# A four-layer state-space image block on one Trainium2 core: z computed beside the layer norm's statistics, the scan's first block made a stage earlier, and y's columns gathered by ScalarE

## The chip, the cores and the metric

The kernel runs on one core of one Trainium2 chip. The metric is the device time of one execution, in microseconds. The kernel before takes 28529.37 us (median of 3 runs, 28515.41 to 28530.03). The times of the profile come from one more, profiled execution of 28593.1 us, whose profiled span is 28591.4 us.

## The reference

Four images of 64 x 64 pixels and 192 channels pass through four layers one after the other. Layers 0 to 2 are selective-scan blocks; layer 3 is a block in which the four directions fall together, so that it needs no scan. For each layer and image, cut to what matters:

```
x  = group_norm(x_in)                        # 32 groups, over the whole image
xi, z = split(x @ in_proj.T)                 # 384 + 384 channels; z = silu(z)
xi = silu(depthwise_conv3x3(xi) + bias)      # layers 1, 2 and 3 alone
# four directions k: rows, columns, rows backwards, columns backwards
dts, B, C = split(x_proj[k] @ xs[k])         # rank + 16 + 16 rows
dt = softplus(dt_proj[k] @ dts + dt_bias[k])
h  = exp(dt * A[k]) * h + (dt * xs[k]) * B   # over 4096 positions, 16 states
y[k] = sum_n h[n] * C[n] + D[k] * xs[k]
y  = y[0] + columns_to_rows(y[1]) + flip(y[2]) + columns_to_rows(flip(y[3]))
y  = layer_norm(y) * w + b                   # over the 384 channels
x_out = x_in + (y * z) @ out_proj.T
```

Everything is float32.

## The kernel before

Channels lie on the partitions, positions along the free axis in 8 chunks of T = 512. The 384 inner channels are three blocks `d` of 128. A loop on the device runs over the 4 images; in it, layer by layer, stand three stages, each ended by a barrier of all engines: `norm_conv`, then `scan`, then `out_gated` (layer 3 has no scan and ends with `out_proj`). So one execution has 16 `norm_conv`, 12 `scan`, 12 `out_gated` and 4 `out_proj`. Each engine's instructions stand in an order written out by hand, and engines wait for each other by counting semaphores; nothing is planned at run time.

`norm_conv` (from L240) takes the group norm's statistics, projects xi (`project_in`, L535), convolves it where there is a convolution (taps on TensorE and VectorE) into `u`, and projects dts, B and C (`project_x`, L558), which ScalarE copies out of PSUM (`keep_x`, L468). SyncE stores them to DRAM: directions 0 and 2 chunk by chunk (`store_even`), directions 1 and 3, transposed, in one go at the end (`store_odd`, L323). SyncE then waits for all of the even stores and for the first chunk's dts, B (`diag`) and C (`c_all`), which it has loaded in the meantime (L359 to L364).

`scan` (from L605) works through 4 directions of 8 chunks of 3 blocks d: 96 units. A unit has 8 steps `g` of 2 states each. In each step TensorE multiplies dt*u with B (`inputs`, L717, into PSUM), ScalarE makes exp(dt*A) (`make_decays`, L842), VectorE runs two scans (`scans`, L918), ScalarE keeps the last column (`keep_last`, L835), GpSimd multiplies with C (`weigh`, L965, waits for `keep_last`), and TensorE sums the product by transposing matmuls (`sums`, L735) three steps later (`PE_LAG`). The next unit's dt is made in between: TensorE's `project_dt` (L697) at g = 1 behind `sums`, ScalarE's `softplus_in` and `softplus_log` at g = 2 and 3, VectorE's `make_dt` after the scans of g = 3, GpSimd's `make_dtu` at g = 3, TensorE's `turn_dtu` (L708) at g = 6, ScalarE's `keep_turned` (L818) at g = 7. The unit before is finished at the same time: `keep_yT` at g = 3, TensorE's `start_y` (L750) at g = 4, `turn_y` at g = 5, ScalarE's `keep_y` (L860) at g = 6. `start_y` adds what y holds so far (an identity matmul over `y_acc`, or in direction 0 the D weights `skip_w` over `u`); in directions 1 and 3 its moving operand is read by columns, 256 bytes from one element to the next. At g = 4 of each chunk's first unit ScalarE issues the two DMAs of `spread` (L826), which bring the next chunk's B into place. Ahead of the first unit stand, in a row: a table load, the three `skip_w` weights (L870), `project_dt`, the softplus, `make_dt`, `make_dtu`, `turn_dtu` and `keep_turned` of unit 0.

`out_gated` (from L986) loads x (two halves), the input weights and the output weights. It first runs the statistics over y's channels: VectorE's `sum_y` and `centre`, TensorE's `mean` (L1011) and `variance` (L1018) by a matmul with a constant matrix, ScalarE's `squares` and `deviation`, GpSimd's sum of squares. z is projected by `project_z` (L1025) on x normalised by ScalarE (`normalise`, L1080); two of the eight chunks lie within the statistics, the other six between the output projections (`project_out`, L1038). ScalarE's `silu` goes from PSUM into `u`, and VectorE's `scale`, `gate` and `add_x` make the result. All `project_out` share one pair of PSUM banks.

## Time and profile before

| what | us |
|---|---|
| median of 3 runs | 28529.37 |
| profiled execution | 28593.1 |
| its profiled span | 28591.4 |
| TensorE matmul busy | 27059.4 (95%) |
| VectorE busy | 25875.7 (91%) |
| GpSimd busy | 23415.0 (82%) |
| ScalarE busy | 18929.7 (66%) |
| one scan of twelve (image 0, layer 0, first to last scan instruction) | 1963.8 |

PE is TensorE's matmul side, PEld its weight load, DVE VectorE, ACT ScalarE, POOL GpSimd, SP SyncE (SPq are the DMAs that it issues). The busy shares are means over stages with different limits, so each stage is to be read by itself. A row of the windows view has the stretch and its length, then the busy time (and instructions) of PE, PEld, DVE, ACT and POOL, the granted TensorE clock, the DMA engines' share and GB/s. A row of the timeline has start, length, engine, line, operation, what it writes and reads, how many in a run, and in brackets how long its engine stood idle and what ended that.

### The profile page before, as it was taken

To read this page: it belongs to the slowest core of one execution; us is meant where nothing else is said; L and a number is where in the kernel's file an instruction comes from. 1 tells how busy PE (TensorE), PEld (TensorE's weight loads), DVE (VectorE), ACT (ScalarE), POOL (GpSimd) and SP (SyncE) were. 2 spreads that over 40 slices of the span, in tenths; PEclk is the share of its full clock that TensorE was granted. 3 is DMA by queue.
4 is the path that set the end of the run, shared out by engine and by line. 5 is a ranking of instruction groups with operands and counts; after the bars stand their busy time and mean duration, and the time that the engine had idled before them with its cause. 6 is when DMAs were issued, how large, how long until landed. Compare 5 with 4: busy or idle time off the path is not lost. (4 is left out here: it accounts for less than half of the span.)

```text
span 28591.4 us, 600844 instructions
## 1 busy us (share of the span) xinstructions
PE 27059.4 (95%) x242880; PEld 20043.6 (70%) x242880; DVE 25875.7 (91%) x24430; ACT 18929.7 (66%) x37728; POOL 23415.0 (82%) x10688
## 2 busy tenths in 40 slices
PE   8999998998999999899899999989989999998998
PEld 6776775774677677577467767757746776775774
DVE  8998997997899899899789989979978998997997
ACT  6775775774677577577467757757746775775774
POOL 7996995994799699599479969959947996995994
PEclk9999999999999999999999999999999999999999
DMA  3332332331333233233133323323313332332331
GB/s 106 102 101 80 105 105 80 106 110 44 101 104 100 82 103 105 80 109 108 45 100 105 99 82 102 105 80 108 108 45 100 105 99 82 102 105 80 108 108 45
DMA packets 3552030, 2679.50 MB, mean 94 GB/s; under 512 B 3255348, under 2 KB 3258636, under 8 KB 3294584
## 3 DMA queue, kind: packets, MB, share of 16 engines
q1 hardware_dynamic: 489912, 2628.56, 25.9%
q10 hardware_dynamic: 3059328, 12.24, 6.2%
q8 instruction: 1934, 31.69, 0.5%
q14 instruction: 856, 7.01, 0.1%
HBM read 2541.99 MB, written 111.15 MB: 93 GB/s over the span
## 5 line engine op out<-in xcount | busy, mean ns | idle before, releaser
L971 POOL TENSOR_TENSOR regB<-regB,regA 128x1024 f32<-128x1024 f32 x9216 | 21517.9, 2376 | 618.8 <-ACT carry L838 607.4
L932 DVE TENSOR_TENSOR_SCAN regB<-regB,carry,ps 128x512 f32<-128x512 f32 x16128 | 19137.1, 1257 | 243.6 <-PE ps L730 215.8
L849 ACT ACTIVATE regB<-regB,a_neg 128x512 f32<-128x512 f32 x18432 | 12184.1, 710 | 0.6 <-issue 0.2
L730 PEld LDWEIGHTS ps<-regA,regB 64*128 64x128 f32 x147456 | 8999.2, 188 | 3536.0 <-issue 2923.7
L730 PE MATMUL ps<-regA,regB 64*128 64x128 f32 x147456 | 10741.4, 285 | 104.7 <-DVE regB L932 59.1
L744 PE MATMUL ps<-ident,regB 128*128 128x128 f32 x73728 | 10082.7, 280 | 229.1 <-POOL regB L971 163.3
L744 PEld LDWEIGHTS ps<-ident,regB 128*128 128x128 f32 x73728 | 7905.5, 141 | 1407.4 <-POOL regB L971 397.9
L838 ACT ACTIVATE carry<-regB 128x2 f32<-128x2 f32 x9216 | 1888.8, 205 | 6151.6 <-DVE regB L932 5617.7
L961 POOL TENSOR_TENSOR regB<-regB,u 128x512 f32<-128x512 f32 x1152 | 1635.0, 1419 | 1972.2 <-DVE regB L915 1972.2
L932 DVE TENSOR_TENSOR_SCAN regB<-regB,ps 128x512 f32<-128x512 f32 x2304 | 2617.4, 1200 | 229.2 <-PE ps L730 193.8
L705 PE MATMUL ps<-regB,dt_w 13*128 13x512 f32 (+1 forms) x2304 | 1274.5, 633 | 171.8 <-SPq L667 171.8
L761 PE MATMUL ps<-pad,ident 128*128 128x512 f32 x1728 | 1376.5, 883 | 8.2 <-ACT regB L858 8.2
L441 DVE SCALAR_TENSOR_TENSOR regB<-pad,vec,regB 128x512 f32<-128x512 f32 x1728 | 1152.8, 744 | 0.0
L910 DVE SCALAR_TENSOR_TENSOR ps<-regB,ps 128x512 f32<-128x512 f32 x1152 | 776.4, 674 | 395.3 <-ACT regB L815 395.3
L864 ACT ACTIVATE pad<-ps 128x512 f32<-128x512 f32 x1152 | 945.3, 821 | 39.0 <-PE ps L767 39.0
L369 POOL MEMSET pad<- 128x198 f32 x12 | 3.2, 265 | 1091.3 <-POOLq L1181 1091.3
L1440 POOL TENSOR_TENSOR regB<-regB 128x512 f32<-128x512 f32 x32 | 44.6, 1395 | 963.0 <-ACT regB L1327 963.0
L915 DVE TENSOR_TENSOR regB<-ps,regB 128x512 f32<-128x512 f32 x1152 | 796.8, 692 | 39.5
L712 PE MATMUL ps<-ident,regB 128*128 128x128 f32 x4608 | 704.1, 276 | 83.5 <-POOL regB L961 82.4
L540 PE MATMUL ps<-regA,regB 96*128 96x512 f32 x1536 | 724.2, 626 | 42.9 <-DMA regB<-w_in_in 28.4
L806 ACT ACTIVATE regB<-ps 128x512 f32<-128x512 f32 x1152 | 676.0, 587 | 122.6 <-PE ps L705 107.0
L568 PE MATMUL ps<-u,regB 128*88 128x512 f32 (+1 forms) x1536 | 698.5, 610 | 47.8 <-ACT u L464 47.8
(103 smaller groups left out, 13630.7 us busy)
## 6 DMA issues: line engine op xcount, KB each, us to landing
regA<-c SPq DMA_DIRECT2D x1536, 1024.0 KB, 4.7
regA<-eye SPq DMA_DIRECT2D x384, 2048.0 KB, 7.7
regA<-x_in SPq DMA_DIRECT2D x16, 1536.0 KB, 13.5
x_keep<-regA SPq DMA_DIRECT2D x8, 3072.0 KB, 17.6
regA<-x_keep SPq DMA_DIRECT2D x16, 1536.0 KB, 13.9
regB<-xd SPq DMA_DIRECT2D x128, 192.0 KB
regB<-w_in_in SPq DMA_DIRECT2D x28, 576.0 KB, 11.5
xd<-regB SPq DMA_DIRECT2D x64, 192.0 KB
```

What stands on the lines that cost most here:

```text
L441: nc.vector.scalar_tensor_tensor(dst, src, wt, part, ALU.mult, ALU.add).then_inc(cv_step, 1)
L705: nc.tensor.matmul(ps[:, Z_BANK, :], dt_w[0:R + 1, k % 2, d * P:(d + 1) * P], dts[0:R + 1], start=True, stop=True).then_inc(z_mm, 1)
L730: mm = nc.tensor.matmul(b.rearrange("p (t s) -> p s t", s=2), dtuT[at, up, q, :], diag[at, cp, q, g], start=True, stop=True)
L744: mm = nc.tensor.matmul(ps[:, Y_BANK + up, at], ring[:, g % RING, s, at], ident[:], start=g == 0 and s == 0 and q == 0, stop=g == PAIRS - ...
L761: nc.tensor.matmul(as_chunk(ps[:, Y_BANK + up, :], k), w, in_order(src, k, d, n), start=True, stop=False)
L838: nc.scalar.activation(carry[:, d, 2 * g:2 * g + 2], ring[:, g % RING, :, T - 1 if c[0] < 2 else 0], ACT.Copy).then_inc(carried, 1)
L849: nc.scalar.activation(decays[:, g % 2, s], dt[:, up, :], ACT.Exp, scale=a_neg[:, c[0], d, 2 * g + s:2 * g + s + 1]).then_inc(a_made, 1)
L864: nc.scalar.activation(in_order(y_acc, k, d, n), as_chunk(ps[:, Y_BANK + up, :], k), ACT.Copy).then_inc(y_kept, 1)
L915: nc.vector.tensor_tensor(dt[:, up, :], ps[:, Z_BANK, :], sp_t[:, 0], ALU.add).then_inc(dt_made, 1)
L932: nc.vector.tensor_tensor_scan(ring[:, g % RING, s, way], decays[:, g % 2, s, way], b[:, s, way], 0.0 if begun else carry[:, d, at:at + 1] ...
L961: nc.gpsimd.tensor_tensor(dtu.rearrange("p (q i r) -> p i q r", i=ROWS, q=QS), dt[:, up, :].rearrange("p (i q r) -> p i q r", i=ROWS, q=QS ...
L971: nc.gpsimd.tensor_tensor(ring[:, g % RING], ring[:, g % RING], c_all[:, g], ALU.mult).then_inc(g_made, 1)
```

## The change

- `scan`, steady work. In directions 1 and 3 a new ScalarE copy, `gather_y`, placed at g = 1, reads y's columns into a contiguous tile `y_col`; `start_y` now takes that tile. The last unit has its own `gather_y` ahead of `keep_yT`. `project_dt` moves ahead of `sums` within g = 1.
- `scan`, its beginning. The first unit's `project_dt`, softplus, `make_dt` and `make_dtu` are moved into the end of `norm_conv`: TensorE's `first_z` ahead of the last `project_x`, ScalarE's `first_softplus` (with a table load in layers 1 and 2) ahead of the last `keep_x`, VectorE's `first_dt` and GpSimd's product behind their other work. The `skip_w` weights are made in unit 0, one per step. SyncE adds what those counts would have been to seven semaphores. The wait for the even stores moves from the end of `norm_conv` to the second chunk (ScalarE), the second step (VectorE) and SyncE's beginning of the scan.
- x's layout becomes two halves one behind the other (`x_of`); its loads and stores go by halves. The first half of x and the weights for z (into `xd_odd`, as `z_w`) are loaded during the scan's last chunk.
- `out_gated`. All eight `project_z` are placed among `mean` and `variance`; ScalarE copies z raw from PSUM into `u` (`keep_z`) and applies `silu` in place after the statistics; VectorE's first four `scale` move in among `centre`; `project_out` uses two pairs of PSUM banks. The next layer's input weights are loaded here, so that `norm_conv` of layers 1 to 3 loads none.
- `out_proj` loses branches that were never taken, and two device loops are unrolled.

```diff
@@ norm_conv, scalar
+                    def first_softplus():
+                        act.wait_ge(z_mm, 1)
+                        if conv:
+                            act.wait_ge(cv_used, (NCH - 1) * NDB)
+                        nc.scalar.activation(sp_t[:, 0], ps[:, FIRST_Z, :], ACT.Relu).then_inc(sp_abs, 1)
+                        nc.scalar.activation(sp_t[:, 1], ps[:, FIRST_Z, :], ACT.Abs).then_inc(sp_abs, 1)
+                        act.wait_ge(sp_abs, 2)
+                        nc.scalar.activation(ps[:, FIRST_Z, :], sp_t[:, 1], ACT.Exp, scale=-1.0).then_inc(sp_exp, 1)
+                        act.wait_ge(sp_exp, 1)
+                        nc.scalar.activation(sp_t[:, 2], ps[:, FIRST_Z, :], ACT.Ln, bias=1.0).then_inc(sp_ln, 1)
@@
+                        if c == NCH and not last:
+                            nc.scalar.preload_act_table_set("natural_log_exp_and_others")
+                            first_softplus()
                         if c:
                             keep_x(c - 1)
@@ norm_conv, tensor
+                    def first_z():
+                        pe.wait_ge(dts_loaded, 16)
+                        pe.wait_ge(w_ready, weights)
+                        pe.wait_ge(pad_made, NCH)
+                        nc.tensor.matmul(ps[:, FIRST_Z, :], dt_w[0:RANK[l] + 1, 0, 0:P], dts[0:RANK[l] + 1],
+                                         start=True, stop=True).then_inc(z_mm, 1)
@@ scan, sync
+                        else:
+                            sp.wait_ge(b_made, S * NDB * PAIRS)
+                            sp.dma_start(xT[:, 0], x_half_of(l, b, 0)).then_inc(x_half0, 16)
+                            sp.dma_start(z_w, w_in[l]).then_inc(zw_loaded, 16)
@@ scan, tensor: start_y
+                        elif k % 2:
+                            pe.wait_ge(col_made, col_unit(c, d) + 1)
+                            nc.tensor.matmul(ps[:, Y_BANK + up, :], ident[:], y_col, start=True, stop=False)
+                            return
@@
-                    first = chunk_of(0, 0, 0)
-                    project_dt(first, 0)
-                    turn_dtu(first, 0)
+                    turn_dtu(chunk_of(0, 0, 0), 0)
@@
                                 inputs(this, d, g, (par + d) % 2, par)
+                                if nxt and g == PE_Z:
+                                    project_dt(*nxt)
                                 if (old := behind(this, before, d, g, PE_LAG)):
                                     sums(*old, par_of(old[0], par, this, old[1]))
-                                if nxt and g == PE_Z:
-                                    project_dt(*nxt)
@@ scan, scalar
+                    def gather_y(c, d):
+                        k, n, _, S = c
+                        if k % 2 == 0:
+                            return
+                        act.wait_ge(y_kept, unit(c, d) - NDB + 1)
+                        act.wait_ge(y_mm, unit(c, d))
+                        nc.scalar.activation(as_chunk(y_col, k), in_order(y_acc, k, d, n), ACT.Copy).then_inc(col_made, 1)
@@
                                 make_decays(this, d, g, (par + d) % 2)
+                                if S == 0 and d == 0 and g < NDB:
+                                    nc.scalar.activation(skip_w[:, g, :], ident[:], ACT.Copy,
+                                                         scale=dsum[:, g:g + 1])
+                                if g == ACT_COL and (old := behind(this, before, d, 0, PAIRS)):
+                                    gather_y(old[0], old[1])
@@ out_gated, tensor
+                    project_z(0)
+                    mean(0)
+                    mean(1)
+                    project_z(1)
+                    mean(2)
+                    mean(3)
+                    variance(0)
+                    project_z(2)
+                    mean(4)
+                    variance(1)
+                    variance(2)
+                    project_z(3)
...
+                    variance(6)
+                    variance(7)
+                    project_z(7)
                     for c in range(NCH):
-                        if c + 2 < NCH:
-                            project_z(c + 2)
                         project_out(c)
@@ out_gated, scalar
+                    def keep_z(c):
+                        act.wait_ge(in_mm, c + 1)
+                        nc.scalar.activation(u_of(c), ps[:, 3 * (c % 2):3 * (c % 2) + NDB, :], ACT.Copy).then_inc(z_kept, 1)
+
                     def silu(c):
-                        act.wait_ge(in_mm, c + 1)
-                        nc.scalar.activation(u[:, :, c * T:(c + 1) * T], ps[:, 3 * (c % 2):3 * (c % 2) + NDB, :],
-                                             ACT.Silu).then_inc(z_made, 1)
+                        act.wait_ge(z_kept, c + 1)
+                        nc.scalar.activation(u_of(c), u_of(c), ACT.Silu).then_inc(z_made, 1)
```

## Rows read from the trace of the kernel before

**Rows 1.** Page, busy us (share of span) and instructions of each engine.
```profile
PE 27059.4 (95%) x242880; PEld 20043.6 (70%) x242880; DVE 25875.7 (91%) x24430; ACT 18929.7 (66%) x37728; POOL 23415.0 (82%) x10688
```

**Rows 2.** Windows: four directions of image 0's first scan; length, then busy per engine.
```profile
153.43:643.44 490.01, 478.31 (x4874) 385.41 (x4872) 480.16 (x432) 352.71 (x740) 473.16 (x215) 0.99 0.36 102
643.44:1137.85 494.41, 492.49 (x4892) 384.70 (x4892) 483.97 (x434) 366.01 (x744) 483.24 (x217) 1.00 0.36 105
1137.85:1624.60 486.75, 479.38 (x4903) 386.39 (x4901) 479.68 (x433) 355.59 (x744) 476.52 (x217) 1.00 0.37 106
1624.60:2117.26 492.66, 490.52 (x4875) 383.51 (x4874) 482.63 (x431) 362.38 (x737) 483.21 (x216) 1.00 0.33 96
```

**Rows 3.** Waits within direction 1: total us, times, longest.
```profile
ACT carry L838 <- DVE regB L932: 115.7, 113, 3.0
...
POOL regB L971 <- ACT carry L838: 11.1, 17, 2.0
DVE regB L932 <- PE ps L730: 9.2, 29, 1.0
```

**Rows 4.** Waits within direction 2.
```profile
DVE regB L932 <- PE ps L730: 6.1, 12, 0.9
```

**Rows 5.** Timeline from the last store of `norm_conv` to the first scan.
```profile
139.50 1.42 SPq L337 DMA_DIRECT2D c<-regA  x1
142.15 1.28 ACT L868 ACT_TABLE_LOAD   x1 [11.00 <-PEq L602]
...
149.51 1.11 PE L712 MATMUL ps<-ident,regB 128*128 128x128 f32 x4 [5.24 <-POOL regB L961]
150.66 0.60 ACT L823 ACTIVATE regB<-ps 128x512 f32<-128x512 f32 x1 [4.00 <-PE ps L712]
...
153.43 1.22 DVE L932 TENSOR_TENSOR_SCAN regB<-regB,ps 128x512 f32<-128x512 f32 x1 [5.32 <-PE ps L730]
```

**Rows 6.** Windows: `out_gated` of image 0: layer 0, in two parts.
```profile
2126.57:2186.97 60.40, 41.31 (x68) 14.65 (x69) 40.76 (x39) 32.62 (x36) 21.53 (x16) 0.78 0.29 67
2186.97:2258.59 71.62, 67.56 (x157) 26.70 (x155) 40.51 (x55) 14.32 (x14) 0.00 (x0) 1.00 0.00 0
```

**Rows 7.** Timeline in a unit of direction 1: start, length, instruction, idle before.
```profile
1016.96 0.20 ACT L838 ACTIVATE carry<-regB 128x2 f32<-128x2 f32 x1 [0.91 <-DVE regB L932]
...
1017.26 1.12 PE L705 MATMUL ps<-regB,dt_w 13*128 13x512 f32 x2
```

**Rows 8.** Timeline, beginning of `norm_conv` in layer 1.
```profile
2263.98 2.92 ACT L450 ACTIVATE regA<-regA,gn_bias,gn_rstd 96x512 f32<-96x512 f32 x4 [0.23 <-DVE gn_bias L401]
...
2266.85 13.48 PE L540 MATMUL ps<-regA,regB 96*128 96x512 f32 x24 [3.62 <-DMA regB<-w_in_in]
...
2268.00 1.28 ACT L509 ACT_TABLE_LOAD   x1
...
2269.29 1.86 ACT L515 ACTIVATE regB<-ident,vec 128x128 f32<-128x128 f32 x6
```

**Rows 9.** Source line L761 (`start_y`), durations in ns (min/median/max): direction 1, direction 0.
```profile
L761 PE MATMUL ps<-pad,ident x38: 1016/1026/1035, 716.1 to 1087.1; 128*128 128x512 f32 x38
...
L761 PE MATMUL ps<-u,pad x40: 592/594/595, 205.7 to 593.1; 128*128 128x512 f32 x40
```

**Rows 10.** Source line L864 (`keep_y`): direction 1 (to columns), direction 0.
```profile
L864 ACT ACTIVATE pad<-ps x20: 1043/1062/1078, 700.0 to 1091.0; 128x512 f32<-128x512 f32 x20
...
L864 ACT ACTIVATE pad<-ps x20: 572/575/577, 210.1 to 597.5; 128x512 f32<-128x512 f32 x20
```

**Rows 11.** Timeline of `out_gated`, layer 0.
```profile
2140.07 1.10 PE L1015 MATMUL ps<-regA,chan_mean 128*128 128x512 f32 x2 [0.27 <-DVE pad L1121]
...
2165.75 5.32 PE L1033 MATMUL ps<-regA,regB 96*128 96x512 f32 x12
...
2179.50 7.64 PE L1033 MATMUL ps<-regA,regB 96*128 96x512 f32 x12 [5.61 <-ACT regA L1086]
```

**Rows 12.** Timeline, beginning of `norm_conv` in layer 2.
```profile
4556.65 0.16 DVE L407 TENSOR_REDUCE dsum<-vec 128x3 f32<-128x12 f32 x1 [13.68 <-issue]
```

More of the change, by code:

```diff
@@ L599, in _ @@
                             project_in(c + 3)
+                        if c == NCH and not last:
+                            first_z()
                         if c:
@@ L1105, in _ @@
+                    silu(1)
+                    keep_z(7)
+                    for c in range(2, NCH):
                         silu(c)
-                        if c + 2 < NCH:
-                            normalise(c + 2)
                 @block.vector
@@ L1307, in _ @@
                     normalise(2, 0)
[L1308 to L1314 removed]
+                    for c in range(1, NCH - 3):
+                        silu(c, c % 2)
+                        normalise(c + 2, c % 2)
                     silu(NCH - 3, 1)
```

332 lines of the change are left out of this document (170 added, 162 removed).

## The prediction

> **What bounds the kernel now.** I read the busy shares first, then windows by direction of a scan, then the waits within them, then timelines at the seams. By the page TensorE is busy 95% of the span, VectorE 91%, GpSimd 82%, ScalarE 66% [rows 1]; with three engines this close the shares don't say which of them a stage waits for. The windows of the first scan do [rows 2]. In directions 1 and 3 TensorE is busy 492.5 of 494.4 us and 490.5 of 492.7 us: it leaves 2 us, so it is the bound. In directions 0 and 2 it leaves 11.7 and 7.4 us, and VectorE (480.2 and 479.7 us) is nearest to the length. An odd direction takes 493.5 us on average, an even one 488.4 us. GpSimd is close behind: 473 to 477 us in even directions, 483.2 us in odd ones, where it too reads u by columns. VectorE's idle time inside a direction is small and names TensorE's `inputs`: 9.2 us in direction 1, 6.1 us in direction 2 [rows 3, 4]. So the scan's steady work, twelve times 1964 us, is near the floor of three engines at once, and can give little. The rest, some 5000 us, has seams where engines stand still: 11.0 us of ScalarE idle at each scan's beginning, and then 11.3 us from 142.15 to the first scan instruction at 153.43 [rows 5]; and `out_gated`, whose 132.0 us hold TensorE work of 108.9 us, much of it at the lower clock [rows 6].
>
> **Beginning of the scan.** Before, unit 0's chain runs alone: 142.15 to 150.66 until `keep_turned` starts, and 2.77 us more to the first scan instruction [rows 5]. After, all up to `make_dtu` lies in the stretch in which SyncE issues the last stores, from the end of the last `keep_x` to 140.92 (139.50 + 1.42), which remains and which waited for nothing else. What is left is the table load or, beside it, about 0.45 us of SyncE's counts (seven, an estimate), then `turn_dtu` of 1.11 us: `keep_turned` can start at about 143.75. That is 6.9 us earlier. The `skip_w` weights, three of 0.3 to 0.4 us (six of the shape take 1.86 us [rows 8]), move into steps 0 to 2, in which ScalarE waits for VectorE; I take 0, at most 1.2 us. Loads of C for the later steps were queued at the stage's start before too, and land before GpSimd comes to them. 12 x 6.9 = 83 us.
> Against it stands what is put ahead of the last `project_x` and `keep_x`. `first_z` costs TensorE 1.12 us [rows 7], 0.9 of it net of overlap; in layer 0 TensorE runs without a gap there, so the stores begin 0.9 us later. In layers 1 and 2 TensorE waits for the last silu, so z is free, but ScalarE has a table load of 1.28 us [rows 8] and four activations of the kind of 0.6 us [rows 5] ahead of the first copy, which is due 2.9 us after the silu: 0.8 us late, of which the stores of layer 1 feel about half. Sum 4 x 0.9 + 4 x 0.4 = 5 us. Net 78 us; from both sides 55 (cover gone in layers 1 and 2, skip weights in full) to 85.
> A table load costs 1.28 us here and the next activation starts 0.01 us behind it [rows 8]. The Trainium skill's "ScalarE: Activation LUTs" (What ACT_TABLE_LOAD costs) adds a drain of 1380 ns to each switch of sets. By that rule the eight loads new in `norm_conv` would each put 1.4 us more ahead of `keep_x`, and the sum would shrink by up to 11 us; the trace doesn't show such a drain.
>
> **Columns gathered by ScalarE.** `start_y` has two passes a unit, 1.026 us each by columns and 0.594 us contiguous [rows 9]: 48 x 0.432 = 20.7 us of TensorE in each odd direction. That doesn't come off the time. VectorE is busy 484.0 us there and GpSimd 483.2 us [rows 2], and even directions with TensorE at 478 us take 488.4 us. Set right with the even ones, an odd direction gains 5.1 us; GpSimd has 8 us more work than there and less time to make good what it loses when ScalarE stands at the spread DMAs, so I take 3.0 us. 24 x 3.0 = 72 us. From both sides: 0 (GpSimd takes TensorE's place) to 24 x 9.5 = 228 us (down to GpSimd's own 483.2 + 1).
> The gather's own length no row shows. Nearest are ScalarE's copy of the same 128x512 to columns, 1.06 us a piece, and contiguous 0.58 us [rows 10]; I take 1.06, it may be up to 1.6 if reading is dearer than writing as on GpSimd. It stands behind step 1's decays. ScalarE waits 115.7 us in 113 pieces for VectorE in direction 1, 1.02 us each [rows 3], and 0.91 us ahead of exactly the `keep_last` that the gather would delay [rows 7]. So `keep_last` comes 0.1 to 0.2 us late, GpSimd is still busy with the product before it, and softplus behind that has the next wait. Cost 0. If that cover were gone, each of the 576 units would pay up to 1.06 us.
> Why a read by columns is slow, "SBUF — State Buffer" of the Trainium skill (Door 1: The DMA port swizzle) says in a note: accesses that leave a 16-byte line pay a penalty, and rows 9 agree. By that rule the penalty moves to ScalarE with the read and is not removed; it speaks against the change where ScalarE has no slack.
>
> **`project_dt` ahead of `sums`.** TensorE's work is the same. Where `sums` waits for GpSimd, z now fills the wait. `sums` comes 1.1 us later, still ahead of `inputs` of g = 2, and the scan that needs both can't tell. Where TensorE waits for GpSimd in step 1 it gains some tenths; VectorE's 6 to 9 us a direction are its limit [rows 3, 4]. I take 10 us in all, 0 to 100.
>
> **End of the scan.** The last `start_y` is on the path, and its two passes lose 0.43 us each [rows 9]; its gather hides behind GpSimd's last product. 12 x 0.87 = 10 us.
>
> **`out_gated`.** Before, from 2186.97 TensorE runs six z and eight outputs in 71.6 us [rows 6]; a block of 12 matmuls takes 5.15 us from start to start, 7.6 us at the lower clock, a mean or variance 1.03 [rows 11]. After, x's half is there. Table load 1.28 and one normalised chunk 1.5: z(0) starts at 2.8 us. The scan's last 10 us leave TensorE mostly idle, so z(0) begins at 1.2 GHz and takes about 8.5 us, as the first 12 of the 24 in 13.48 us do in `norm_conv` [rows 8]: 11.3. Then seven z (36.1), sixteen means and variances (16.5), and waits that I trace: mean(1) for centre(0) 1.8, mean(3) for centre(2) 1.8, variance(2) and variance(7) for deviation 0.8 and 1.1. That is 69.4. ScalarE behind variance(7): deviation 1.3, table 1.3, two silu 2.9, `keep_z(7)` 1.45, which is 1.8 after z(7)'s end: 71.2. Eight outputs on two pairs of banks, no wait for `add_x`: 41.2 (VectorE has gate 2.1 and add_x with statistics 2.5 per chunk, below 5.15). The last sum 0.2 + 1.2: 113.8 us. Against 132.0 that is 18.2 us; one more block at the lower clock costs 2.3 us [rows 11], and I allow half: 17. 12 x 17 = 204 us. From both sides: 8 us a stage (each handover waits twice as long, two blocks at the lower clock) to 24 (no wait, full clock).
>
> **`norm_conv` without the weights' load.** In layer 1 the first projection waits for the weights until 2266.85; the normalised chunk was there at 2265.5: 1.4 us [rows 8]. Layer 3 and 0 don't wait. In layer 2 VectorE waits to 4556.65 for `vec` and `dt_w` [rows 12], which holds back the pad's filling by up to 4.7 us; with 0.6 MB less ahead in the queue I take 2. 4 x 1.4 + 4 x 2 = 14 us, 0 to 25. x's stores in halves: 0, within 2 us each way for four images.
>
> **Sum.** 78 + 72 + 10 + 10 + 204 + 14 = 388 us off the profiled execution's 28593.1: 28205. The median of the runs is 63.7 us below that execution, so I forecast 28141 us, 1.36% less. A measurement of this kernel tells about 0.2% (57 us) from no change.
>
> **Rivals.**
> 1. GpSimd takes TensorE's place in odd directions. For: 483.2 us busy, and it alone waits for ScalarE's `keep_last`, 11.1 us in direction 1 [rows 3]. Against: even directions reach 486.8. The 72 us are lost: 28213 us.
> 2. The reverse: the odd directions fall to GpSimd's floor, 9.2 us each, since z's new place and the freed TensorE end the stalls together. Against: GpSimd's waits of 10 us in both kinds of direction come from the spread, which stays. 28141 - 149 = 27992 us.
> 3. `out_gated` gives half. z(0) stands ahead of mean(0), so VectorE's statistics stand still for 8 us, and mean and centre follow each other one by one; gaps may hold the clock at 1.2 GHz. For: the first part of the stage had a granted clock of 0.78 [rows 6]. 8.5 us instead of 17: 28243 us.
> 4. Slower: the gather outlasts ScalarE's wait in odd units. Then `keep_last` is late, GpSimd idles, and VectorE stops at the ring's end. It decides from a gather over about 1.9 us (two waits of 0.9 to 1.0), and once ScalarE is the bound the full 1.06 us comes on all 576 units: +611, and the 72 are gone: 28141 + 72 + 611 = 28824 us.
>
> **Chances.** Forecast 0.60, its own range 28050 to 28240; rival 1 0.13, rival 2 0.08, rival 3 0.13, rival 4 0.03, other mixtures 0.03. Rivals 1 and 3 together give 28315, rival 2 with the upper bounds elsewhere 27950. Range 27980 to 28300, leaving out 2 in 10. All cases but rival 4 and part of the mixtures are faster by more than 57 us: faster 0.96, same 0.01, slower 0.03.
>
> **What would show it.** Scan: first scan instruction 4.4 us after the stage's start instead of 11.3; `start_y` at 0.594 us in all directions; odd directions near 490.5 us with TensorE at about 475 and idle; the gather near 1.06 us with ScalarE still waiting for VectorE before each `keep_last`. `out_gated` near 115 us, with no TensorE gap over 2 us after the first z, and outputs 5.15 us apart. `norm_conv` of layer 1 shorter by 1 us. I am wrong if odd directions keep 493 us, if `out_gated` stays above 120 us, or if ScalarE's waits for VectorE in odd directions vanish.

## The result: 28001 us instead of 28523 us, and the profile after

| | before | changed |
|---|---|---|
| median, same chip (4 runs each) | 28523.11 us | 28001.17 us |
| lowest to highest | 28515.41 to 28530.03 | 27996.4 to 28006.58 |
| profiled span | 28591.4 | 27996.2 |

The ratio is 0.9816, 95% interval 0.9801 to 0.983: 522 us less. The forecast was 28141 us (range 27980 to 28300). So the side and the range held (the lower bound by 21 us), but 140 us more came off than forecast, and the time lies outside the forecast's own range of 28050 to 28240. The profiled execution of before lies 70 us above the median of its runs and that of the changed kernel 3 us below, so the two traces differ by 595 us; about 70 us of that do not belong to the change, and they lie in the scan's steady work, as a second trace of the changed kernel shows below.

Stage by stage (from the two traces, sums over the 16, 12, 12 and 4 stages, each up to the next stage's start): `norm_conv` −24, `scan` −375, `out_gated` −196, `out_proj` 0 us.

The page of the changed kernel, its engine line and three of its groups, which answer to [rows 1]. In a group's row stand line, engine, operation, tiles, count, then busy time and mean ns, then idle time of the engine ahead of them and what ended it:

```profile
PE 26574.5 (95%) x242880; PEld 20088.3 (72%) x242880; DVE 25757.7 (92%) x24430; ACT 19561.3 (70%) x38408; POOL 23396.5 (84%) x10688
...
L1066 POOL TENSOR_TENSOR regB<-regB,regA 128x1024 f32<-128x1024 f32 x9216 | 21500.3, 2381 | 552.5 <-ACT carry L925 540.9
L1029 DVE TENSOR_TENSOR_SCAN regB<-regB,carry,ps 128x512 f32<-128x512 f32 x16128 | 19038.5, 1256 | 90.9 <-PE ps L813 82.3
...
L925 ACT ACTIVATE carry<-regB 128x2 f32<-128x2 f32 x9216 | 1886.0, 205 | 5506.4 <-DVE regB L1029 4956.7
```

The shares hardly moved (TensorE stays at 95%); they could not have told what happened. TensorE lost 485 us of work, ScalarE gained 632.

**The four directions of the first scan** (windows view, columns as in [rows 2]), changed kernel:

```profile
145.95:633.50 487.55, 478.77 (x4874) 386.61 (x4872) 480.01 (x432) 353.40 (x742) 472.81 (x215) 0.99 0.37 108
633.50:1117.57 484.07, 477.06 (x4897) 385.38 (x4896) 479.35 (x434) 385.37 (x767) 481.83 (x217) 1.00 0.37 106
1117.57:1601.57 484.00, 477.97 (x4897) 385.97 (x4896) 479.10 (x434) 356.12 (x745) 476.90 (x217) 1.00 0.37 107
1601.57:2084.73 483.16, 474.78 (x4875) 383.68 (x4874) 478.73 (x431) 382.13 (x760) 481.53 (x216) 1.00 0.35 102
```

Against [rows 2] look at the second and fourth row: 494.41 has become 484.07 and 492.66 has become 483.16. In the second row GpSimd is busy 481.83 of 484.07 us (before 483.24 of 494.41), while TensorE has 7 us over. The bound of an odd direction has changed hands, from TensorE to GpSimd. And the odd directions are now no slower than the even ones, which the prediction had taken as their limit.

**The waits in directions 1 and 2**, to be held against [rows 3] and [rows 4] (total us, times, longest):

```profile
ACT carry L925 <- DVE regB L1029: 86.1, 91, 2.2
...
DVE regB L1029 <- PE ps L813: 3.7, 6, 0.8
POOL regB L1066 <- ACT carry L925: 2.2, 5, 0.6
```

```profile
POOL regB L1066 <- ACT carry L925: 6.7, 9, 1.4
...
DVE regB L1029 <- PE ps L813: 4.0, 7, 0.8
```

GpSimd's waits for ScalarE in direction 1 fell from 11.1 us to 2.2, VectorE's for TensorE from 9.2 to 3.7.

**The gather in a unit of direction 1** (ScalarE's timeline), the same place as [rows 7], and the durations of the gather and of `start_y`'s new pass (source view, ns min/median/max), which answer to [rows 9, 10]:

```profile
1016.99 0.20 ACT L925 ACTIVATE carry<-regB 128x2 f32<-128x2 f32 x1 [0.91 <-DVE regB L1029]
1017.10 1.32 ACT L936 ACTIVATE regB<-regB,a_neg 128x512 f32<-128x512 f32 x2
1018.32 1.08 ACT L954 ACTIVATE xd_odd<-pad 128x512 f32<-128x512 f32 x1
1019.33 0.20 ACT L925 ACTIVATE carry<-regB 128x2 f32<-128x2 f32 x1
```

```profile
L954 ACT ACTIVATE xd_odd<-pad x23: 1077/1089/1099, 654.2 to 1098.9; 128x512 f32<-128x512 f32 x23
...
L842 PE MATMUL ps<-xd_odd,ident x46: 592/594/595, 663.2 to 1107.6; 128*128 128x512 f32 x46
```

`keep_last` at 1019.33, which answers to the one at 1016.96 in [rows 7], has no idle time ahead of it any more: the gather filled the wait of about 0.9 us. TensorE's pass went from 1026 to 594 ns, and ScalarE pays 1089 ns.

**The beginning of the scan** (timeline), to be held against [rows 5]:

```profile
138.85 1.59 SPq L357 DMA_DIRECT2D c<-regA  x1
141.62 1.28 ACT L964 ACT_TABLE_LOAD   x1 [9.46 <-PEq L670]
...
142.02 1.11 PE L795 MATMUL ps<-ident,regB 128*128 128x128 f32 x4 [10.91 <-SPq L743]
143.17 0.60 ACT L908 ACTIVATE regB<-ps 128x512 f32<-128x512 f32 x1 [0.27 <-PE ps L795]
...
145.95 2.33 DVE L1029 TENSOR_TENSOR_SCAN regB<-regB,ps 128x512 f32<-128x512 f32 x2 [16.32 <-PE ps L813]
```

From the table load to the first scan instruction it is 4.33 us now, 11.28 before, and 4.32 to 4.33 in all twelve scans.

**`out_gated` of layer 0**: its window, then rows of ScalarE's and TensorE's timeline, against [rows 6, 11]:

```profile
2095.79:2210.08 114.29, 102.24 (x224) 41.02 (x224) 80.71 (x94) 57.95 (x58) 22.03 (x16) 0.96 0.09 22
```

```profile
2095.79 1.28 ACT L1206 ACT_TABLE_LOAD   x1 [0.93 <-PEq L1077]
...
2097.08 2.93 ACT L1194 ACTIVATE regA<-regA,gn_bias,gn_rstd 96x512 f32<-96x512 f32 x4
...
2098.65 8.37 PE L1125 MATMUL ps<-regA,xd_odd 96*128 96x512 f32 x12 [4.86 <-ACT regA L1194]
...
2106.86 1.02 PE L1107 MATMUL ps<-regA,chan_mean 128*128 128x512 f32 x2
...
2165.72 43.11 PE L1139 MATMUL ps<-pad,regB 128*96 128x512 f32 x96 [1.84 <-ACT u L1200]
```

The stage takes 114.3 us instead of 132.0. (The mean over the twelve stages, each up to the next stage's start, is 117.1 us instead of 133.5.) The first z starts 2.86 us in and takes 8.37 us; the eight outputs run as one block of 96 matmuls in 43.11 us without a gap.

### The profile page after: what moved, and what is told of

Its sections match the earlier page's. It is cut to its first block and busy times, and to the rows that moved or that the text cites. A ratio compares the mean times of both kernels' runs of the same rounds, so it can differ in the third digit from the quotient of the medians.

```text
span 27996.2 us, 601988 instructions
## 1 busy us (share of the span) xinstructions
PE 26574.5 (95%) x242880; PEld 20088.3 (72%) x242880; DVE 25757.7 (92%) x24430; ACT 19561.3 (70%) x38408; POOL 23396.5 (84%) x10688
## 5 line engine op out<-in xcount | busy, mean ns | idle before, releaser
L945 ACT ACTIVATE regB<-ps 128x512 f32<-128x512 f32 x1152 | 681.6, 592 | 46.2 <-PE ps L827 46.2
L900 ACT ACTIVATE regB<-ps 128x512 f32<-128x512 f32 x1140 | 682.3, 598 | 36.2
## 6 DMA issues: line engine op xcount, KB each, us to landing
regA<-x_in SPq DMA_DIRECT2D x16, 1536.0 KB, 11.5
```

## The experiments

They ran in three groups, each on a chip of its own with runs of the kernel before beside it: medians 28601.33 us (the four on z's place and the gather), 28594.26 (gather doubled and tripled, spread on SyncE, mean first) and 28598.39 (the rest), so alike for these three chips and 0.3% above the first measurement's. The last group repeats the changed kernel; it is the measure for all, and stands first. Differences to "the changed kernel" are to this repeat, whose chip reads within 4 us of the others for the kernel before. Below, the directions' means are the four directions of a scan, in us, from first to first scan instruction, averaged over the twelve scans of a trace: 488.9, 495.2, 488.4, 491.0 before, and 485.5, 485.3, 485.2, 482.8 in the changed kernel's first trace. One stage of `out_gated` alone can mislead (layer 0's first one takes 114.3 us in the first trace of the changed kernel and 117.0 in the second, at granted clocks of 0.96 and 0.92), so its mean over the twelve stages, each up to the next stage's start, is given beside it: 133.5 us before, 117.1 and 117.3 in the changed kernel's two traces.

**The changed kernel again** (no edit).

> The changed kernel once more, as the measure for the other three on the same chip. Both theories: ratio to the kernel before 0.9816, within the interval of the first measurement (0.9801 to 0.983). A ratio outside it would mean that the ratios of the experiments cannot be compared across chips at the size of 40 us.

Measured: 28078.33 us, ratio 0.9818 (0.9803 to 0.9833). The ratio carries over, as both theories said; the time does not: both kernels are 0.3% slower here. The directions' means are 487.9, 486.7, 486.9, 483.7; summed over the twelve scans that is 219 us below before, where the first trace of the changed kernel was 296 below. So some 219 us are the change's. The other 77 us can be found: ScalarE's DMA issues of `spread` last 1461 us in all in this trace, 1444 in the trace of before, 1441 to 1476 in every other trace in which ScalarE makes them, and 1384 in the changed kernel's first trace. Per scan, that first trace has 2.5, 1.3, 1.9 and 0.8 us less of these issues in directions 0 to 3, and its directions are 2.4, 1.4, 1.7 and 0.9 us shorter. So the changed kernel's first trace and the trace of before differ by some 60 us of DMA issues besides the change. The other stages agree (`out_gated` −194, `norm_conv` −27, beginnings −83).

**The scan's two edits, undone singly and together.** z behind `sums` again:

```diff
                                 inputs(this, d, g, (par + d) % 2, par)
-                                if nxt and g == PE_Z:
-                                    project_dt(*nxt)
                                 if (old := behind(this, before, d, g, PE_LAG)):
                                     sums(*old, par_of(old[0], par, this, old[1]))
+                                if nxt and g == PE_Z:
+                                    project_dt(*nxt)
```

> The changed kernel with project_dt behind sums again, the rest as changed. The changed kernel took 28001 us. By the prediction's term z's new place is worth 10 us: 28010. Theory A (each of the two edits frees TensorE at the place where VectorE's stall is made, and the gather's freed time does most of it): 28020 to 28060, odd directions still near 484 us in image 0's first scan. Theory B (z's new place is what brought the unforecast 200 us): 28150 to 28250, with VectorE's stall ahead of the scans of g = 2 back at 0.5 us in second units of even directions.

No gather; `start_y` reads by columns again:

```diff
-                        elif k % 2:
-                            pe.wait_ge(col_made, col_unit(c, d) + 1)
-                            nc.tensor.matmul(ps[:, Y_BANK + up, :], ident[:], y_col, start=True, stop=False)
-                            return
@@ gather_y
-                        if k % 2 == 0:
+                        if True:
                             return
```

> The changed kernel with start_y reading y's columns itself and no gather, z ahead of sums kept. Prediction's term: 82 us slower (72 for the directions, 10 for the tails): 28083. Theory A: 28150 to 28230, odd directions at 491 to 494 us, since TensorE has 20.5 us of work in each 20.5 us unit and is the bound there again. Theory B: 28020 to 28060.

Both edits together:

> The changed kernel with both undone: what is left are the scan's beginning, out_gated and norm_conv. If the scan's steady work is the whole of the unforecast part, this takes 28523 less 83 (beginnings), 196 (out_gated) and 24 (norm_conv), so 28220 us, with even directions at 488 and odd ones at 493 us. If the beginnings brought something into the steady work as well, it is below 28190.

| kernel | us | ratio (95%) | directions' means |
|---|---|---|---|
| both edits undone | 28290.0 | 0.989 (0.9874 to 0.9907) | 488.8, 494.8, 488.7, 491.3 |
| gather undone | 28264.09 | 0.9881 (0.9864 to 0.9897) | 488.0, 495.1, 487.5, 490.9 |
| z's place undone | 28131.26 | 0.9837 (0.9821 to 0.9854) | 487.9, 488.3, 488.8, 483.9 |
| changed | 28078.33 | 0.9818 (0.9803 to 0.9833) | 487.9, 486.7, 486.9, 483.7 |

With both undone the directions are those of before, and 311 us are still gained: that is what the scan's beginnings, `out_gated` and `norm_conv` are worth (303 by the changed kernel's first trace: 83 + 196 + 24; 291 by this kernel's own: 83 + 189 + 19). The two edits of the steady work make the remaining 212 us. The gather alone makes 159 (28290.0 − 28131.3), all of it in the odd directions, 7 us each; z's place alone 26, none of it in odd directions, as TensorE is their bound there whatever the order; z's place on top of the gather 53. The prediction had 72 and 10. Applied to the first measurement's 28523 us, the ratios give 28058 us with z's place undone and 28184 with the gather undone, both as theory A had them. The ratios' intervals are some 45 us wide on each side, but the 26 us are a difference on one chip, where the four runs of either kernel don't overlap (28248 to 28269 and 28279 to 28300). The 53 compare two chips. For them the traces speak: the scan's steady work, summed over the twelve scans, is 23388 us with z's place undone and 23339 to 23351 in five traces that have z ahead of `sums` and at most one gather per unit (this repeat, and below the kernels with the gather left out, with the mean first, with x loaded late and with one pair of banks), 37 to 50 us less. Direction by direction the differences of about 1 us are no larger than those between two traces of one kernel. That z's place is worth more with the gather than without it (53 against 26) rests on one trace and the medians, and is likely but not certain.

The windows of directions 1 and 3 of the first scan without the gather show it: TensorE is back at 492.55 of 495.11 us.

```profile
637.47:1132.58 495.11, 492.55 (x4892) 384.71 (x4892) 484.09 (x434) 364.64 (x744) 482.86 (x217) 1.00 0.36 104
...
1619.14:2111.37 492.23, 490.33 (x4875) 383.53 (x4874) 482.56 (x431) 361.29 (x737) 482.70 (x216) 1.00 0.35 100
```

**What the gather costs.** 46 of a scan's 48 gathers are left out, and `start_y` reads the contiguous tile as it stands (y of these units is not computed):

```diff
-                            pe.wait_ge(col_made, col_unit(c, d) + 1)
+                            pe.wait_ge(col_made, k // 2 + 1)
@@ gather_y
-                        if k % 2 == 0:
+                        if k % 2 == 0 or n or d:
                             return
```

> The changed kernel with the gather made only for the first unit of each odd direction; 46 of 48 copies a scan are left out and start_y reads the old tile, so y of these directions is not computed. It tells the gather's own price. Prediction: 0 (ScalarE's wait hides it): 28001 plus or minus 15. Rival: keep_last is late by part of the gather and GpSimd pays: 30 to 100 us faster than the changed kernel.

Measured: 28073.74 us, ratio 0.9816 (0.98 to 0.9832). 5 us from the changed kernel, on another chip, and 6 us in the traces' steady work: the gather has no cost that shows. In the page the same can be read from ScalarE's idle time ahead of `keep_last`: 6077 us without the gathers, 5575 in the changed kernel's second trace. The 552 gathers left out last 601 us; each puts off the next activation by about 1.0 us (1018.32 to 1019.33 above), 550 us in all, and 502 of these came out of that wait.

Then the gather doubled, and tripled (copies into a free part of its buffer, in all chunks of the odd directions but a scan's last two):

```diff
+                        for e in range(1 if c[3] < K * NCH - 2 else 0):   # tripled: range(2 ...)
+                            nc.scalar.activation(as_chunk(xd_odd[:, (1 + e) * T:(2 + e) * T], k), in_order(y_acc, k, d, n), ACT.Copy)
                         nc.scalar.activation(as_chunk(y_col, k), in_order(y_acc, k, d, n), ACT.Copy).then_inc(col_made, 1)
```

> The changed kernel with one more copy of y's columns by ScalarE per unit of directions 1 and 3, into an unused tile. Times are compared by their ratio to the kernel before on the same chip (changed kernel 0.9816), since the same kernel differs by 0.3% from chip to chip. Rival 4's mechanism says the cover is ScalarE's two waits of 0.9 to 1.0 us: two copies of 1.0 just fit, so 0 to 60 us more (0.982 to 0.984). If only the one wait beside the gather's place covers it, each of 572 units pays near 1 us: 500 us more, 0.999.

> The same with two more copies, three in all: 3.0 us of ScalarE beside a cover of 1.9. By the mechanism ScalarE is now late by 1 us where softplus and the decays of g = 2 and 3 follow; it comes good at g = 5 (2.2 us of wait). If GpSimd's backlog hides that, 50 to 150 us more than the changed kernel; if it reaches VectorE through the decays, 300 to 600 us more.

Measured: doubled 28166.91 us, ratio 0.9851 (0.9835 to 0.9868), +89 us on the changed kernel; tripled 28427.81, ratio 0.9941 (0.9924 to 0.9957), +350 us. Over the 504 units that have them, the first extra copy costs 0.18 us a unit and the second 0.52. The tripled one's timeline in a unit of direction 1 has three gathers in a row, and `keep_last` only at 1018.69, without a wait ahead of it. Below it stand the waits of its direction 1 (total us, times, longest):

```profile
1015.70 2.08 ACT L955 ACTIVATE xd_odd<-pad 128x512 f32<-128x512 f32 x2
...
1017.69 1.09 ACT L956 ACTIVATE xd_odd<-pad 128x512 f32<-128x512 f32 x1
...
1018.69 0.19 ACT L925 ACTIVATE carry<-regB 128x2 f32<-128x2 f32 x1
```

```profile
POOL regB L1068 <- ACT carry L925: 20.4, 41, 2.2
DVE regB L1031 <- PE ps L813: 15.4, 26, 1.8
...
DVE regB L1031 <- ACT regB L936: 5.5, 9, 0.8
```

In the changed kernel's second trace the first two of these waits are 3.9 and 5.1 us. So the chain of rival 4 (`keep_last` late, GpSimd idle, VectorE stopped) exists at three gathers, and VectorE now also waits for the decays, a way that rival 4 did not name. Its threshold lies between one gather (1.09 us, free) and two (2.1 us, 0.18 us a unit), where "about 1.9 us" fits, but its price does not hold: even the second extra copy costs half of its length, not all of it. The doubled gather's 89 us fall between the two theories (up to 60, or 500), the tripled one's 350 us in the range of a delay that reaches VectorE (300 to 600). ScalarE's idle time ahead of `keep_last` fell again, from 5575 to 5010 us. That further waits in the unit take the rest is my reading.

**What is late now.** The two DMAs of `spread` go to SyncE's queue, ScalarE issues none:

```diff
@@ scan, sync
+                            sp.wait_ge(spread_b, S * ROWS * 16 + ROWS * 16)
+                            spread_rows(sp, l, after[0], after[1], 1 - par, spread_b)
                             load_dts(after)
@@ scan, scalar
-                                if d == 0 and after and g == ACT_B:
-                                    spread(after, 1 - par)
```

> The changed kernel with the two spread DMAs of each chunk issued by SyncE at the beginning of its step, instead of by ScalarE at g = 4. Theory C: ScalarE stands 3.5 to 4.4 us at these issues once a chunk, keep_last and then GpSimd, TensorE and VectorE are late, and that is what is left of VectorE's stalls. Then units fall to 20.10 us in even directions (VectorE's work) and 20.17 in odd ones (GpSimd's): 100 to 180 us less than the changed kernel, ratio 0.975 to 0.978. Rival: SyncE is blocked in its turn and its loads of dts and C come late, or the issue is not what stalls: 0 or slower.

Measured: 27816.61 us, ratio 0.9727 (0.971 to 0.9743), about 260 us less than the changed kernel; theory C holds, but its 100 to 180 us were too few. The means of the four directions are 480.8, 481.4, 480.8, 481.0. What it removes, in the changed kernel's direction 2 (ACTq is ScalarE's queue issuing; then ScalarE, and below GpSimd):

```profile
1185.39 3.66 ACTq L240 DMA_DIRECT2D eye<-b  x1
1185.61 0.72 ACT L936 ACTIVATE regB<-regB,a_neg 128x512 f32<-128x512 f32 x1
1189.09 0.20 ACT L925 ACTIVATE carry<-regB 128x2 f32<-128x2 f32 x1 [2.76 <-issue]
```

```profile
1189.44 2.38 POOL L1066 TENSOR_TENSOR regB<-regB,regA 128x1024 f32<-128x1024 f32 x1 [0.94 <-ACT carry L925]
```

The second issue lasts 3.66 us, ScalarE stands idle for 2.76 us of it, `keep_last` starts only 0.04 us behind its end, and GpSimd stands 0.94 us. That happens about once a chunk: direction 2 has eight chunks, and GpSimd waits nine times for `keep_last` in it, 6.7 us in all. With the spread on SyncE the directions 1 and 2 of the first scan read:

```profile
627.11:1108.48 481.37, 477.54 (x4897) 385.85 (x4896) 478.55 (x434) 385.19 (x767) 481.37 (x217) 1.00 0.38 107
1108.48:1589.15 480.67, 477.03 (x4897) 386.17 (x4896) 478.53 (x434) 355.50 (x745) 477.02 (x217) 1.00 0.39 107
```

GpSimd is busy 481.37 us of 481.37 in direction 1: that is the floor of an odd direction. In direction 2 VectorE is nearest, with 478.53 of 480.67 us. It also shows why even directions were not the limit of the odd ones. The even directions stood 7 us above their length here and the odd ones 4 us, and the ScalarE pair of issues takes 4.2 us a chunk in even and 3.7 in odd directions (means of the changed kernel's second trace).

**The order at `out_gated`'s head.** `mean(0)` ahead of `project_z(0)`:

```diff
-                    project_z(0)
                     mean(0)
+                    project_z(0)
                     mean(1)
```

> The changed kernel with mean(0) ahead of project_z(0) in out_gated, all else as changed. It tests the prediction's term that z(0) in front costs mean(0) and mean(1) their waits (8 us during which VectorE stands still, 1.8 us of TensorE): z(0) starts 0.7 us later, mean(1) needn't wait. By the working out_gated is 1.1 us shorter, 13 us in all; by rival 3 (statistics held up are what bounds the stage) 3 to 6 us shorter each, 36 to 72 us.

Measured: 28036.29 us, ratio 0.9803 (0.9786 to 0.9819); `out_gated` 111.3 us in layer 0, 113.8 on average, 3.5 us less a stage (−43 us over twelve, by the traces). The working had expected 13 us in all and rival 3, by which held-up statistics bound the stage, 36 to 72: the size is rival 3's. A mean in the stream takes 1.02 us. TensorE's timeline at the head says why:

```profile
2102.06 1.55 PE L1107 MATMUL ps<-regA,chan_mean 128*128 128x512 f32 x2 [3.52 <-DVE regA L1253]
2103.41 6.71 PE L1125 MATMUL ps<-regA,xd_odd 96*128 96x512 f32 x12
```

The mean fills the time in which ScalarE still loads its table and normalises: z(0) starts no later (2.87 us in, where it was 2.86). And the granted clock is back at 0.99 from 5.5 us into the stage:

```profile
2103.50:2106.00 2.50, 2.50 (x4) 1.08 (x4) 2.35 (x2) 1.83 (x3) 0.00 (x0) 0.50 1.06 242
2106.00:2110.00 4.00, 4.00 (x11) 1.75 (x10) 0.70 (x2) 0.92 (x1) 2.52 (x2) 0.99 0.97 223
```

In the changed kernel it was still 0.50, the lower of the two levels (1.2 GHz), until 7.2 us in, and 0.80 on average up to 11.2:

```profile
2098.65:2103.00 4.35, 4.35 (x5) 1.85 (x6) 0.00 (x0) 1.36 (x2) 0.00 (x0) 0.50 1.03 247
2103.00:2107.00 4.00, 4.00 (x9) 1.76 (x8) 0.00 (x0) 0.00 (x0) 0.00 (x0) 0.80 1.02 240
```

So z(0) takes 6.71 us instead of 8.37, and the pair of z(0) and mean(0) is done 9.6 us into the stage instead of 12.1: 2.5 us, of which 1.7 are z(0)'s shorter time and 0.8 the mean that now fills idle time. The last 1 us a stage I have not traced; rival 3's held-up statistics can be in it.

**x and z's weights not loaded ahead.**

```diff
@@ scan, last chunk, sync
-                            sp.dma_start(xT[:, 0], x_half_of(l, b, 0)).then_inc(x_half0, 16)
-                            sp.dma_start(z_w, w_in[l]).then_inc(zw_loaded, 16)
@@ out_gated, sync
+                    sp.dma_start(xT[:, 0], x_half_of(l, b, 0)).then_inc(x_half0, 16)
+                    sp.dma_start(z_w, w_in[l]).then_inc(zw_loaded, 16)
                     sp.dma_start(xT[:, 1], x_half_of(l, b, 1)).then_inc(x_half1, 16)
```

> The changed kernel, but the first half of x and the weights for z are loaded at the beginning of out_gated instead of in the scan's last chunk. Theory (z beside the statistics pays only because x is there): the first project_z stands at the head of TensorE's list and now waits for the load and the first normalise, some 8 to 10 us of landing time less what the statistics need anyway; mean(0) and all behind it come that much later: out_gated 122 to 126 us instead of 114.3, some +100 to +140 us in all, ratio to the kernel before about 0.986. Rival (the order of out_gated's work alone gives the gain, the preload nothing): the load lands before it is missed or the lost time is made good behind the statistics: out_gated stays within 2 us of 114.3, ratio 0.9816 to 0.982.

Measured: 28221.48 us, ratio 0.9864 (0.9849 to 0.9879), +143 us, where 100 to 140 were expected; `out_gated` 124.8 us, 127.9 on average. TensorE's first z starts 12.8 us in, and its idle time ends with the weights' landing:

```profile
2109.61 2.90 PE L1125 MATMUL ps<-regA,xd_odd 96*128 96x512 f32 x3 [14.78 <-DMA xd_odd<-w_in_in]
```

So the preload is worth 10.6 us a stage by the means; the other edits keep 5.6 us of 16.2 without it.

**One pair of PSUM banks for the outputs.**

```diff
-                        wait(pe, res_made, c - 1)
+                        wait(pe, res_made, c)
...
-                                    ps[0:CB, 2 * (c % 2) + cb, :], out_w[:, d, cb * CB:(cb + 1) * CB],
+                                    ps[0:CB, cb, :], out_w[:, d, cb * CB:(cb + 1) * CB],
```

> The changed kernel, but all eight project_out share one pair of PSUM banks again, so each waits until add_x has read the one before. Theory of the prediction (no wait for add_x is a term of the gain): each of seven outputs starts about 1.4 us later than the end of the one before, out_gated 124 us instead of 114.3, +120 us over the twelve stages, ratio about 0.986. Rival (the second pair is worth nothing, because the outputs wait for VectorE's gate anyway): out_gated within 2 us of 114.3, ratio 0.9816 to 0.982.

Measured: 28232.59 us, ratio 0.987 (0.9855 to 0.9885), +154 us, where 120 were expected; `out_gated` 125.9 us, 128.8 on average. Each output now waits for `add_x`:

```profile
2192.77 5.36 PE L1139 MATMUL ps<-pad,regB 128*96 128x512 f32 x12 [1.40 <-DVE regA L1283]
2199.53 5.36 PE L1139 MATMUL ps<-pad,regB 128*96 128x512 f32 x12 [1.40 <-DVE regA L1283]
```

6.76 us from start to start instead of 43.11 / 8 = 5.39: seven times 1.4 us, 10 us a stage. By the means the stage is 11.5 us longer; the other 1.5 us I have not traced. Each of the two (preload, second pair) is worth over half of the stage's whole gain, and they don't stand in for each other.

**The best of both: spread on SyncE and the mean first.**

> The changed kernel with two edits together: the two DMAs of spread are issued by SyncE instead of ScalarE, and mean(0) stands ahead of project_z(0). Theory (the two act in different stages and add up): 255 + 40 us less than the changed kernel, ratio to the kernel before 0.9727 - 0.0013 = 0.971, units of the scan at 20.1 us in all four directions and out_gated near 111.5 us. Rival (SyncE's later issues crowd the load of x and of z's weights, which lie in the scan's last chunk, so that out_gated gives some back): out_gated 113 us or more, ratio 0.9725 or above.

Measured: 27771.71 us (27766.17 to 27783.2, 5 runs), ratio 0.9711 (0.9698 to 0.9724), against 0.9818 for the change alone. Both gains are there (directions 480.7, 481.6, 480.9, 481.3; `out_gated` 109.1 to 111.7 us), and SyncE's added issues hold back neither the load of x nor that of z's weights so far that `out_gated` would show it: the rival's 113 us or more did not come. It is the fastest kernel of this study, 827 us under before on the same chip.

## Why the prediction was right, and where it was short

Term by term; the measured sum is that of the medians (522 us).

| term | forecast | measured | from |
|---|---|---|---|
| scan beginnings, gross | 83 | 83 | 12 × 6.95, traces |
| odd directions (gather) | 72 | 159 | both undone, less z's place undone |
| z ahead of `sums` | 10 | 26 alone, 53 with the gather | the four kernels |
| end of the scan | 10 | −4 to +1 | two traces |
| `out_gated` | 204 | 194 to 196 | two traces |
| `norm_conv`, net | 14 − 5 = 9 | 24 to 27 | two traces |

- **Beginnings.** Right in place and size: 4.33 us against "4.4". `turn_dtu` starts 0.40 us into the stage, beside the table load, where 0.45 were estimated for SyncE's counts. The stage starts 1.2 us behind the last store, as before, and no later than before.
- **`out_gated`.** Right: 114.3 us against the 113.8 worked out; z(0) at 2.86 us (2.8) and 8.37 us long (8.5), outputs 5.39 us apart (5.15; 2 us too little for eight, made good elsewhere in the stage). Over twelve stages it gained 16.2 us each, where 17 were forecast. The block of 7.64 us that was read as one at the lower clock [rows 11] had a granted clock of 0.71 on average, so it was a mixed one. Rival 3's size (half of the gain lost) is refuted by the traces; its cause, z(0) ahead of mean(0), does cost 3.5 us a stage, more than half of that by the clock and idle time at the head. The preload and the second pair are each shown by an experiment to be needed.
- **Table load.** At 2095.79 ScalarE's table load takes 1.28 us, and the activation behind it starts 0.01 us after its end, at 2097.08. The drain that the Trainium skill's "ScalarE: Activation LUTs" (What ACT_TABLE_LOAD costs) adds is not there in this trace either. (The stage's second load, at 2160.13, starts 0.02 us behind the activation ahead of it, and the next activation 0.01 us behind the load.)
- **Odd directions: the term that was mis-sized.** The mechanism was right: TensorE was the bound, and the gather took it away. The gather's own length came out at 1.09 us where 1.06 was taken. (The upper bound of 1.6 leaned on GpSimd: its product takes 1552 ns with u read by columns and 1274 without; no run shows GpSimd writing by columns.) The step that failed is "Set right with the even ones, an odd direction gains 5.1 us ... so I take 3.0". It took the even directions' 488.4 us as the floor that three engines make together. It is no floor: with ScalarE's DMA issues gone both kinds run at 481 us. The even ones lose 7 us to the spread, the odd ones 4, so an odd direction that TensorE no longer bounds goes *below* the even ones: 493.1 to 486.1 us by the gather alone, 485.2 with z's place. That is rival 2's picture for the most part (8 of its 9.2 us per odd direction; GpSimd busy 481.8 of 484.1), and its 27992 us lie 9 us from the measured time, the forecast 140. That closeness is in part luck: the odd directions gave 87 us more than the forecast's 72 where rival 2 had 149 more, and z's place and `norm_conv` made up the rest. Rival 2 was given 0.08 with the argument that GpSimd's waits come from the spread, "which stays". The spread stayed, but in direction 1 its effect on GpSimd shrank from 11.1 us [rows 3] to 2.2 (3.9 in the second trace; with the spread on SyncE no such wait is left): the wait was counted as belonging to the spread alone, while part of it was time that GpSimd could not make good as long as it also waited for TensorE's pace. This last point, why the wait shrank, is my reading of the traces; no experiment parts the two.
- **z ahead of `sums`.** Within its bounds (0 to 100), three to five times the value taken. It was priced by VectorE's waits in directions 1 and 2, some of which went. That TensorE's work is the same and the gain comes from waits was right; the size was not.
- **End of the scan.** The gather at the end hides, as said; but the term is not there. GpSimd is now the last: its last product ends 3.4 us behind VectorE's last scan instruction where it was 2.66 us before (all twelve scans of each trace), which takes 0.76 of the 0.87 us back, and the clock goes with the rest: from the last scan instruction to `out_gated` it is 8.8 us at best and up to 11.1, in ten of twelve scans over 9 (before 8.9 to 10.6). In the first scan's end TensorE waits for GpSimd, its granted clock falls to 0.50, and the two passes take 2.07 us:

```profile
2088.21 1.97 PE L827 MATMUL ps<-ident,regB 128*128 128x128 f32 x8 [1.21 <-POOL regB L1066]
...
2090.86 2.07 PE L842 MATMUL ps<-xd_odd,ident 128*128 128x512 f32 x2 [0.69 <-ACT regB L945]
```

```profile
2090.80:2093.00 2.20, 2.13 (x4) 1.00 (x5) 0.00 (x0) 0.01 (x1) 0.00 (x0) 0.50 0.00 0
```

- **`norm_conv`.** In layer 1 the projection starts 4.72 us into the stage, 6.01 before: 1.3 us of the 1.4 forecast, of which 0.4 remain, as the new work at the end takes the rest. Layer 2 gave 17.5 of the 24 us in the first trace. There VectorE's wait went from 13.68 to 11.71 us, the 2 us forecast [rows 12], but the stage won 4.4: the convolution starts 2.1 us earlier, and its first blocks run with more of the higher clock (4.49 and 5.31 us where they took 5.46 and 5.70, at granted clocks of 0.61 and 1.00 instead of 0.50 and 0.93). Together that is 3.5 us of the 4.4 in the stage read here; the clock was the part left out:

```profile
4463.27 4.49 PE L607 MATMUL ps<-pad,regB 128*128 128x512 f32 x6 [3.29 <-ACT pad L494]
4467.60 5.31 PE L595 MATMUL ps<-regA,regB 96*128 96x512 f32 x12
```

  Another 3.9 us of the 24 are layer 3's, whose stage takes 141 us in some images and 143 to 144 in others in both kernels, so they may be chance.

- **Rival 1** (GpSimd takes TensorE's place and nothing is gained) had the right engine and the wrong consequence: GpSimd is nearest to the length of the odd directions now, but at 484 and not at 493 us. **Rival 4** is excluded for one gather; its chain shows at three, at half its price.
- Of what would have made me wrong, nothing came: odd directions left 493, `out_gated` is under 120, and ScalarE's waits in direction 1 fell to 86.1 us but did not vanish.

## What to carry to other kernels

When one engine's work is taken off a stage, the new floor to reckon with is the busy time of the next engine (here GpSimd, 481 us, reached only once the spread had left ScalarE) and not the length of a sister stage: first ask what keeps the sister above its own busiest engine. A wait of about 1 us that recurs at one place of every unit could be filled here with work of that length for nothing, and past it the price rose (0.18, then 0.52 us per added copy of 1.1 us); double and triple the work to find where. DMA issues on a compute engine's queue belong in the list of its work even though they don't count as busy.

## What the hardware showed that was not expected

- Two DMA issues on ScalarE's queue left ScalarE idle for 2.76 us ahead of its next activation (the pair takes 3.5 to 4.2 us on average by direction); on SyncE's queue the same pair takes 5.3 to 5.7 us and no engine is seen to wait for it. That is worth 260 us of 28000 here.
- Reading one and the same 128x512 tile by columns costs TensorE 0.43 us more per pass than reading it contiguously (1026 and 594 ns). ScalarE's copy of it takes 1.09 us, 0.5 more than its contiguous copy out of PSUM (0.58); two passes share one copy, so it is also less work.
- z's first block after a pause took 8.37 us, and 6.71 us when one mean of 1.55 us ran ahead of it.
- Three chips ran the kernel before at 28594 to 28601 us, the first at 28523, 0.3% less. The changed kernel's two traces differ by 77 us in the scan's steady work and by 76 us in the time of ScalarE's DMA issues, direction by direction alike; that these issues are what differs between the chips is likely by that, but no run shows it apart. The changed kernel's ratio agreed on the two chips on which it was measured (0.9816 on the first, 0.9818 on one of the three).
